# Two small reorderings in an attention and mixture-of-experts kernel: where a score maximum and an output tile stand in two engines' orders

## What is computed

```python
x = x + attention(layernorm(x), ctx, ctx, wq, wk, wv, wo)     # 4 batches of 512 tokens, width 512
x = x + moe(layernorm(x), gate_w, gate_up, down, shared...)   # 2048 tokens, 64 experts, 6 of them per token
# attention: k = concat(ctx, x' wk^T), v = concat(ctx, x' wv^T); softmax(q k^T / sqrt(512)) v wo^T, no mask
# moe: scores = softmax(x' gate_w^T); top 6 of 64; each expert takes its first 128 token slots
#      silu(x' Wg) * (x' Wu) then Wd, scaled by the score, added back to its tokens; one shared expert for all
```

## Time and profile before

| what | value |
|---|---|
| plain runs, median of 3 | 786.0 us (784.77 to 786.11) |
| profiled execution, first to last instruction (its span) | 793.0 us |
| profiled execution, its own time with what lies around the span | not given |
| TensorE matmuls | 756.5 us busy, 95% |
| VectorE | 604.0 us, 76% |
| ScalarE | 448.9 us, 57% |
| GpSimd | 304.6 us, 38% |
| mean granted TensorE clock | 0.988 |
| moved by transfers | 187.68 MB, mean 237 GB/s |

### The profile page before, as it was taken

How to read it: one execution, slowest core, us unless ns; L and a number is a source line. 1 busy time by engine, 2 the same in 40 slices (tenths; PEclk the granted TensorE clock), 3 DMA queues, 4 the chain that set the end, 5 groups by cost and what they waited for, 6 DMA issues and landing times.

```text
span 793.0 us, 10834 instructions
## 1 busy us (share of the span) xinstructions
PE 756.5 (95%) x3766; PEld 636.3 (80%) x3766; DVE 604.0 (76%) x1194; ACT 448.9 (57%) x795; POOL 304.6 (38%) x255
## 2 busy tenths in 40 slices
PE   7999999999999999999999999999999999989983
PEld 5887878877788777877888898988888898877772
DVE  6558666786668766765577799999999999989622
ACT  4424333333334333435153799999998999989710
POOL 2000010544105440055324255556666666656440
PEclk9999999999999999999999999999999999999997
DMA  5933564625666346243385899999999999999988
GB/s 175 280 59 107 172 226 167 147 109 164 233 199 160 116 142 257 102 109 117 116 340 195 315 325 359 357 343 345 352 347 349 348 350 345 350 345 353 217 172 202
DMA packets 86244, 187.68 MB, mean 237 GB/s; under 512 B 26016, under 2 KB 32544, under 8 KB 82592
## 3 DMA queue, kind: packets, MB, share of 16 engines
q1 hardware_dynamic: 54688, 141.84, 49.7%
q0 software_dynamic: 18480, 39.93, 21.7%
q10 hardware_dynamic: 13024, 5.25, 2.8%
HBM read 143.33 MB, written 42.87 MB: 235 GB/s over the span
## 4 chain that ended last, share of the span: by engine, by line
PE 51%; DMA 13%; issue 9%; POOL 9%; DVE 9%; ACT 4%; ACTq 2%; another core or an unknown queue 1%; SPq 0%; POOLq 0%; DVEq 0%
PE bank L1239 8%; PE bank L1240 8%; PE bank L1241 8%; DMA second_sum<-eo,idx_all 4%; POOL out_rows L1500 3%; DMA second_sum<-product,idx_all 3%; POOL second_sum L1500 3%; PE scores L1239 2%; PE scores L1241 2%; PE scores L1240 2%; PE ps_gu L1239 2%; PE ps_gu L1241 2%; PE ps_gu L1240 2%; POOL xg L1492 2%; PE ps_dn L1239 2%
## 5 line engine op out<-in xcount | busy, mean ns | idle before, releaser
L495 POOL DMA_INDIRECT table<-rows,slot x72 | 82.3, 1143 | 155.8 <-DVEq L977 112.4
L1635 DVE TENSOR_TENSOR gu_lo<-raw,gu_hi 128x768 fp32r<-128x768 f32 x126 | 120.2, 955 | 8.7 <-ACT gu_hi L1543 6.8
L1543 ACT ACTIVATE gu_hi<-raw 128x768 fp32r<-128x768 f32 x128 | 107.3, 841 | 0.0
L1239 PE MATMUL ps_gu<-gu_hi,xgT_hi 128*128 128x384 f32 x256 | 91.4, 357 | 0.0
L1241 PE MATMUL ps_gu<-gu_hi,xgT_lo 128*128 128x384 f32 x256 | 86.3, 337 | 0.0
L1240 PE MATMUL ps_gu<-gu_lo,xgT_hi 128*128 128x384 f32 x256 | 86.1, 336 | 0.0
L526 ACT ACTIVATE qT<-bank 128x512 fp32r<-128x512 f32 x32 | 19.1, 597 | 111.7 <-PE bank L1241 70.2
L1492 POOL DMA_INDIRECT xg<-x_rows,idx_all x39 | 46.1, 1183 | 47.2 <-PE ps_xgT L1771 20.8
L531 ACT ACTIVATE pbuf<-scores,negmax 128x1024 f32<-128x1024 f32 x16 | 17.8, 1115 | 71.0 <-DVE negmax L727 60.3
L669 DVE TENSOR_TENSOR qT<-bank,qT 128x512 fp32r<-128x512 f32 x32 | 22.0, 689 | 43.5 <-ACT qT L526 32.8
L1500 POOL DMA_INDIRECT out_rows<-product,idx_all x24 | 40.5, 1688 | 23.0 <-DMA out_rows<-eo,idx_all 11.3
(11 more groups left out here) (299 smaller groups left out, 2201.7 us busy)
## 6 DMA issues: line engine op xcount, KB each, us to landing
raw<-expert_in SPq DMA_DIRECT2D x64, 1024.0 KB
rest<-rest_in SPq DMA_DIRECT2D x32, 256.0 KB
x_rows<-pbuf SPq DMA_DIRECT2D x17, 256.0 KB, 2.1
stage<-wkT_in SPq DMA_DIRECT2D x4, 1024.0 KB
stage<-ctxT_in SPq DMA_DIRECT2D x4, 1024.0 KB
stage<-wvT_in SPq DMA_DIRECT2D x4, 1024.0 KB
stage<-ctx_in SPq DMA_DIRECT2D x4, 1024.0 KB
stage<-woT_in SPq DMA_DIRECT2D x4, 1024.0 KB
```

Of the source, the lines that this page charges most:

```text
L495: pool.indirect_dma_start(out=table, out_offset=bass.IndirectOffsetOnAxis(ap=slot[:, i, k:k + 1], axis=0), in_=rows[:, i, k, :], in_offset ...
L1239: pe.matmul(out, still[0], moving[0], start=first, stop=False)
L1543: act.activation(gu[n % GU_SLOTS][0][part], gate_up_of(n, part), ACT.Copy).then_inc(weights_high, 1)
L1635: return dve.tensor_tensor(lo, x, hi.bitcast(F32), ALU.subtract)
```

## The change

In ScalarE's and VectorE's bodies of batches 0 to 2, the split of av 3 moves from behind the four pieces of moved rows to ahead of them, directly behind av 2. For the last batch the two stood side by side already. On VectorE, the maximum of score tile 2 is taken at the start of the body in batch 0 alone; for batches 1 to 3 it is taken in the body before, in the second half of the routes, behind the increment that gives back the bank of positions and ahead of the small slot operations.

```diff
--- before.py
+++ after.py
@@ -556,15 +556,14 @@
             h(("av", 1))
             if more:
                 high_item(b, more, "ctxT'")
-                h(("av", 2))
+                h(("av", 2), ("av", 3))
                 for a in range(QUADS):
                     act.wait_ge(xnT_moved[a], (b + 1) * 16 * QUADS)
                     hi, lo = tokens_of(a)
                     act.activation(hi, plain(lo), ACT.Copy).then_inc(xnT_high, 1)
             else:
                 high_item(b, more, "su")
-                h(("av", 2))
-            h(("av", 3))
+                h(("av", 2), ("av", 3))
             if more:
                 high_item(b, more, "wq'")
             else:
@@ -834,7 +833,8 @@
                 dve.tensor_scalar(x2[:, i, :], res[:, i, :], mv2[:, i, 0:1], rstd2[:, i:i + 1],
                                   ALU.subtract, ALU.mult).then_inc(x2_ready, 1)
 
-            maximum(b, 2)
+            if not b:
+                maximum(b, 2)
             low_item(b, more, "ctx")
             maximum(b, 3)
             for part in range(4):
@@ -865,7 +865,7 @@
             l(("av", 1))
             if more:
                 low_item(b, more, "ctxT'")
-                l(("av", 2))
+                l(("av", 2), ("av", 3))
                 for a in range(QUADS):
                     dve.wait_ge(xnT_high, b * QUADS + a + 1)
                     hi, lo = tokens_of(a)
@@ -873,8 +873,7 @@
             else:
                 low_item(b, more, "su")
                 dve.tensor_scalar(value, tok[:, :], -float(T), None, ALU.add)
-                l(("av", 2))
-            l(("av", 3))
+                l(("av", 2), ("av", 3))
             if more:
                 low_item(b, more, "wq'")
             else:
@@ -966,6 +965,8 @@
                             op0=ALU.is_equal, op1=ALU.mult, accum_out=posk[:, i, k:k + 1])
                 link(last)
                 dve.nop().then_inc(group_taken, 1)
+                if n == 1:
+                    maximum(b + 1, 2)
 
                 dve.tensor_scalar(over[:, two, :], posk[:, two, :], float(CAP), OVER, ALU.is_ge, ALU.mult)
                 link(dve.scalar_tensor_tensor(out=slotf[:, two, :], in0=posk[:, two, :], scalar=float(E),
```

## The result

The changed kernel takes 789.17 us (median of 8 runs, 788.08 to 790.2) against 786.06 (8 runs, 784.77 to 788.21): a ratio of 1.003, 95% interval 1.002 to 1.0041. It is 3.1 us slower. Timed once more beside the experiments it took 788.64 against 786.35, ratio 1.0029 (1.0014 to 1.0044). Of the 29 runs of the kernel before beside that timing, one took 836.16 us at a granted clock of 0.848, and the ratio leaves it out. The forecast was 788.0.

What follows compares the result with a forecast made beforehand. TensorE was taken to bound the first batch and DMA the expert phase, attention delays passing through. Moving the maximum gives 0, moving output 3 plus 2.1, rounded to 2.0, on 786.0: 788.0 us; own range 786.9 to 789.0, wide 783.5 to 789.2.

Steps and rivals of the forecast that it cites:

- The stops: VectorE and ScalarE in the attention phase: idle some 2 to 4 us, mostly belonging to the profiled execution, absent in plain runs.
- the five long waits: TensorE ahead of the exponentials' transposes (1.54, 0.95, 1.58 us) and the output projections (1.03, 1.41): 6.51 us hanging on VectorE's and ScalarE's idle stretches.
- The argument from 793.0 against 786.0: Profiled span exceeds the plain median by at least 7.0 us, close to TensorE's 6.51 us of waits; the expert phase could hold it.
- The prediction's sentence on the records' pipeline: Profiler notification queue: its pipeline pushes back instead of losing records and can throttle an engine; no row shows it.
- Part one at 0: Third maximum moved earlier on VectorE, batches 1 to 3: worth 0 in a plain run, as ScalarE's eight DMA issues end later.
- The slip of wq': ScalarE, batches 0 to 2: 2.19 us of row copies fall between output 3 and wq', which starts 2.1 us later.
- The slack of 1.22 us: VectorE's idle time ahead of q 1's split swallows the rest of the 2.1 us; 0.8 us per batch comes through.
- the 0.1 us credited at the projection's fourth part: TensorE's fourth part of the first projection: gain of 0.1 us from earlier output 3, leaving net plus 0.7 per batch.
- plus 3 us if q 0 and q 1 slip by 1.0 us each time: VectorE's splits ahead of TensorE's x2T transposes: a softer case in which the sum becomes plus 3.
- the third rival: Later x2T splits hold back wv's load, v 0 up to 0.4 us later per batch: plus 3.2, 789.2 us; chance 0.05.
- The stops as a lasting thing: VectorE's and ScalarE's idle stretches occur in plain runs too, so the change gains 2.1 us: 783.9 us; chance 0.28.
- The slip swallowed whole: VectorE's chain has more slack in a plain run, so wq's delay costs nothing within noise: 786.4 us; chance 0.17.

Runs made afterwards that it cites:

- the kernel before, looked at again: The kernel before with no edit, profiled again and timed as its own control: 786.13 us, ratio 1.0005 (0.9993 to 1.0018).
- part one's 0.9993: Against the kernel before, only the maximum of score tile 2 moved, the attention outputs left as before: 785.99 us, ratio 0.9993 (0.998 to 1.0006).
- two pieces behind: Against the kernel before, output 3 split between the second and third of the four row pieces, maximum left as before: 786.25 us, ratio 1.0005.

## Why the prediction was right, and where it was off

*The stops.* The step that took the five long waits for part of one execution held, and with it the sign: nothing was there to be gained. The argument from 793.0 against 786.0 pointed the right way, and the doubt beside it, that the expert phase could hold the 7 us, is answered: the attention phase held 7.7 of 8.0. That the profiled execution as such brings them was one word too much: eleven other profiled executions of this case have none. Nothing here tells what stopped VectorE, ScalarE and GpSimd in that one. The prediction's sentence on the records' pipeline found no support in a run.

*Part one at 0.* Right, by its own step: ScalarE's eight issues are last, not the maximum.

*The slip of wq'.* 2.1 us forecast, 2.09 measured, from ScalarE's four row copies that lost their cover.

*The slack of 1.22 us.* Right as a mechanism: the lengths bend at 1.18. The cost per batch was put at 0.8 less 0.1, so 0.7, and measured at 0.91, 0.94 and 0.94 in the batches 0 to 2 (lengths of 18.53, 18.50 and 18.50 us before, 19.44 in all three after). Two terms were mis-sized. The wait stands ahead of the third x2T group already and not the last: q 0's bank is late first, TensorE stands 0.98 us for it, and the length shows 0.91 to 0.94 where the sum had 0.8. And the 0.1 us credited at the projection's fourth part was not there: the kernel before, looked at again, has no wait there in any batch. The three lengths add up to 2.8 us where the sum had 2.1. The path moved by 2.6 and 3.0 us in the two looks at the changed kernel. The prediction had named this case, plus 3 us if q 0 and q 1 slip by 1.0 us each time, but not as its centre.

*The range.* The first median, 789.17, lies 0.2 us above the forecast's own range (786.9 to 789.0) and inside the wide one (783.5 to 789.2) by 0.03 us, only because that took in the centre of the third rival, whose mechanism did not happen. That is luck. The second, 788.64, lies in the own range. The chances hold an error of sums as well: four fifths of 0.50 is 0.40, where 0.36 was put.

*The rivals.* The stops as a lasting thing (783.9 us) fell with the second look at the kernel before and with part one's 0.9993. The slip swallowed whole (786.4) would have needed 0.9 us more slack. With a slip that the slack does cover, two pieces behind, the time is 786.25. The longer slip through wv' (789.2) gave about the right time for the wrong reason: no profile shows a wait ahead of v 0, and the three lengths hold 2.8 of the 3.0 us.

*Pass-through.* The medians fit that the expert phase gives nothing back: the path is 3.0 and 2.6 us longer, the times 3.1 and 2.3 us. Single profiles can't show it: from the same point to the end they take anything from 430.6 to 436.7 us, a spread of 6 us without relation to the edits. The 436.7 is part one's, which costs nothing.

## What to carry to other kernels

An operation that waits for nothing in its old place may be standing in another wait's idle time. Put behind that wait, it delays the next thing on the engine by nearly its whole length: here 2.2 us of row copies made a slip of 2.1 us, to bring forward a piece whose own lateness had cost nothing. Before an edit is built on a wait, look at a second execution of the same kernel: the largest waits of one profile (1.0 to 1.6 us each) were not in any other. And a slack can be measured: add a copy of known length in front of the suspected link and see from where on the path follows. The path in the profile is the finer measure: here it gave the slips of 0.4 us per batch to about 0.1 us, while medians of ten runs were off by up to 1 us.

## What was not expected

One of twelve profiled executions had stops of 2.3 to 4.4 us on three engines and a span of 793.0 us; the others' spans run from 782.8 to 790.3 over kernels whose medians differ by up to 5 us. Its stops stand where table scatters and moves of blocks run side by side, but these do so in every execution. What made them was not tried. They are rare: the 106 times of the kernel before that the ratios rest on lie between 784.0 and 790.51 us, and this execution's span alone was 793.0.
